# First layer of a retention network with routed experts: the layer-norm rows of four items are written straight into the token rows' place, and GpSimd's two passes over them move four steps later

## The reference

```
xn = layernorm(x)
h = xn
for l in range(4):
    k, q, v = split(h @ Wkqv[l]);  r = tril(q k^T / sqrt(d)) / row_norm;  r = r / clip(|sum r|, 1)
    a, gate = split((r @ v) @ Wm1[l] + bm1[l]);  m = groupnorm(a * silu(gate) @ Wm2[l] + bm2[l])   # per item
    y = m + h
    h = layernorm(gelu(y @ Wf1[l] + bf1[l]) @ Wf2[l] + bf2[l] + y) * ln_g[l] + ln_b[l]
expert = argmax(softmax(xn @ gate_w));  g = weight * (gelu(xn @ w1[e] + b1[e]) @ w2[e] + b2[e])
out = x + h * silu(g)
```

## Time and profile before

| | |
|---|---|
| median of 3 runs | 507.23 us (507.22 to 507.36) |
| the profiled execution | 506.84 us |
| its span | 504.9 us |
| TensorE busy | 469.9 us (93%) |
| VectorE busy | 383.9 us (76%) |
| ScalarE busy | 253.4 us (50%) |
| GpSimd busy | 259.6 us (51%) |
| the multiply L483, 31 times | 42.5 us, 1.37 us each |
| the add L487, 31 times | 41.8 us, 1.35 us each |
| scatters L471, 32 times | 32.5 us, 1.02 us each |

### The profile page before, as it was taken

One profiled execution on the slowest core, in us unless ns is written; L12 is line 12 of the kernel. 1 busy time (PEld: TensorE's weight loads), 2 busy tenths in 40 slices (PEclk: granted clock), 3 DMA queues, 4 the chain that ended last, 5 costly groups with the idle time before them and its releaser, 6 DMA issues.

```text
span 504.9 us, 9876 instructions
## 1 busy us (share of the span) xinstructions
PE 469.9 (93%) x3157; PEld 392.3 (78%) x3157; DVE 383.9 (76%) x1342; ACT 253.4 (50%) x533; POOL 259.6 (51%) x285
## 2 busy tenths in 40 slices
PE   6999889999999999999999999999999999999751
PEld 4887666766889888988888898889888988767431
DVE  4768887788867767777787677777767777889986
ACT  3823334444566554565655446656554565455320
POOL 4520188888454455544545554544455556445542
PEclk9999999999999999999999999999999999999896
DMA  9998411111611111110111111111111000510022
GB/s 264 236 127 204 174 38 39 34 37 58 130 60 43 58 44 59 59 65 31 49 49 51 53 63 59 59 38 38 59 43 59 33 12 6 152 27 1 26 79 62
DMA packets 47345, 35.05 MB, mean 69 GB/s; under 512 B 13320, under 2 KB 38736, under 8 KB 47296
## 3 DMA queue, kind: packets, MB, share of 16 engines
q1 hardware_dynamic: 44496, 28.94, 22.1%
q0 software_dynamic: 2272, 4.71, 2.8%
q10 hardware_dynamic: 528, 0.79, 0.5%
HBM read 14.70 MB, written 9.42 MB: 48 GB/s over the span
## 4 chain that ended last, share of the span: by engine, by line
PE 65%; POOL 12%; DVE 11%; issue 6%; DMA 2%; ACT 1%; POOLq 0%; SPq 0%; DVEq 0%; ACTq 0%
PE bank L1272 8%; PE bank L1199 7%; PE bank L1183 7%; POOL x_slots L471 6%; PE pair L1346 4%; PE pair L1318 4%; PE bank L1210 4%; PE pair L1300 4%; PE bank L1359 4%; PE bank L1211 4%; PE bank L1212 4%; PE pair L1348 3%; PE pair L1298 3%; POOL ln_rs L426 2%; PE bank L1254 2%
## 5 line engine op out<-in xcount | busy, mean ns | idle before, releaser
L483 POOL TENSOR_TENSOR zhat<-zhat,all_lg 128x512 f32<-128x512 f32 x31 | 42.5, 1373 | 88.1 <-PE bank L1244 74.1
L1272 PE MATMUL bank<-all_f,G_sb 128*128 128x128 f32 x512 | 74.2, 278 | 0.0
L656 ACT ACTIVATE y_sb<-bank,gn_bi,gn_sc 128x512 f32<-128x512 f32 x32 | 24.9, 778 | 97.3 <-DVE gn_bi L1050 97.3
L1272 PEld LDWEIGHTS bank<-all_f,G_sb 128*128 128x128 f32 x512 | 68.6, 195 | 1.4 <-issue 1.4
L651 ACT ACTIVATE uT_h<-bank 128x512 fp32r<-128x512 f32 x32 | 19.1, 597 | 97.5 <-PE bank L1254 97.5
L426 POOL TENSOR_TENSOR ln_rs<-ln_ve,half_neg 128x4 f32<-128x4 f32 x32 | 33.4, 1045 | 34.7 <-DVE ln_ve L680 34.4
L1183 PEld LDWEIGHTS bank<-moe_w,h_T 128*128 128x128 f32 x312 | 39.5, 191 | 13.8 <-issue 13.8
L568 ACT ACTIVATE h_T<-bank,w_t 128x128 f32<-128x128 f32 x156 | 44.5, 372 | 5.1 <-PE bank L1199 5.1
L523 POOL DMA_INDIRECT y_rows<-yt,slot_info x39 | 40.9, 1049 | 11.0 <-POOL yt L520 11.0
L636 ACT ACTIVATE G_sb<-bank,all_par 128x512 f32<-128x512 f32 x64 | 43.0, 694 | 7.1 <-PE bank L1235 4.7
L503 POOL TENSOR_TENSOR gn_rs<-gn_ve,half_neg 128x1 f32<-128x1 f32 x32 | 18.5, 578 | 51.4 <-DVE gn_ve L898 51.3
(11 more groups left out here) (178 smaller groups left out, 1241.3 us busy)
## 6 DMA issues: line engine op xcount, KB each, us to landing
w_t<-moe_w SPq DMA_DIRECT2D x39, 258.0 KB, 2.4
x_slots<-moe_w SPq DMA_DIRECT2D x1, 2515.5 KB, 21.6
xt<-x_slots SPq DMA_DIRECT2D x39, 64.0 KB, 1.8
x_sb<-in_L_attn_x SPq DMA_DIRECT2D x8, 256.0 KB, 5.7
moe_w<-in_L_ffn_w SPq DMA_DIRECT2D x1, 2048.0 KB, 19.0
moe_w<-y_rows SPq DMA_DIRECT2D x8, 256.0 KB, 4.6
out<-moe_w SPq DMA_DIRECT2D x7, 256.0 KB, 2.3
all_f<-in_L_attn_Wf SPq DMA_DIRECT2D x2, 512.0 KB, 4.3
```

The source lines that it names most:

```text
L483: pool.tensor_tensor(zhat[:, b % 2, :, :], zhat[:, b % 2, :, :], all_lg[:, li, :].unsqueeze(1).broadcast_to([P, C, D]), ALU.mult)\
L1272: last = mm(bank[7][:, at_c], G_sb[:, k, at_c], all_f2[:, li, k, :], start=False, stop=k == 1)
```

## The change

For items 0 to 3 (`ASIDE`), VectorE and ScalarE write the normalised rows into the item's own place in htok, where TensorE transposes them from (`zhat_rows`). GpSimd's multiply is then in place in htok, and so is the add. These four items' passes leave steps 3 to 6; step 7 has those of items 0 and 4, step 8 of 1 and 5, step 9 of 2 and 6, step 10 of 3 and 7, from step 11 on all is as it was. As htok is made in another order, the waits on its semaphore count by `htok_made`. The three splits of Wf1 leave step 7: each of steps 8, 9 and 10 does one, behind the layer norm's power. Nothing of the computation is altered.

```diff
+        ASIDE = 4
+        HTOK = [k for b in range(ASIDE) for k in (b, ASIDE + b)] + list(range(2 * ASIDE, LB))
+        def htok_made(n):
+            return HTOK.index(n) + 1
+        def zhat_rows(n, b):
+            return htok[:, b * C:(b + 1) * C, 0:D] if n < ASIDE else zhat[:, b % 2, :, :]
...
+            def token_rows(n, b, li):
+                if n < LAST_LAYER:
+                    pool.wait_ge(pe_zT, n + 1)
+                else:
+                    pool.wait_ge(z_done, n + 1)
+                z = zhat_rows(n, b)
+                pool.tensor_tensor(z, z, all_lg[:, li, :].unsqueeze(1).broadcast_to([P, C, D]), ALU.mult)\
+                    .then_inc(hg_done, 1)
+                pool.wait_ge(hg_done, htok_made(n))
+                pool.tensor_tensor(htok[:, b * C:(b + 1) * C, 0:D], z,
+                                   all_lb[:, li, :].unsqueeze(1).broadcast_to([P, C, D]), ALU.add)\
+                    .then_inc(htok_done, 1)
             def step(l, t):
                 first = l == 0
+                s = l * B + t
+                if 0 <= s - (B - 1) < ASIDE:
+                    token_rows(s - (B - 1), s - (B - 1), 0)
                 w = at(l, t, 3, B, LB)
-                if w and w[0] != LB - 1:
...
+                if w and w[0] >= ASIDE and w[0] < LB - 1:
+                    token_rows(*w)
...
-                if first and t == B - 1:
-                    for k in range(1, L - 1):
-                        split_f1(k)
...
-                if first and t == B - 1:
-                    split_f1(L - 1)
+                if l == 1 and t < L - 1:
+                    split_f1(t + 1)
...
-                        last = act.activation(zhat[:, b % 2, c, :], bank[7][:, c * D:(c + 1) * D], ACT.Identity,
+                        last = act.activation(zhat_rows(n, b)[:, c, :], bank[7][:, c * D:(c + 1) * D], ACT.Identity,
...
-                    need(dve, htok_done, n - 1)
+                    if n >= ASIDE + 2:
+                        dve.wait_ge(htok_done, htok_made(n - 2))
...
-                        last = dve.tensor_scalar(zhat[:, b % 2, c, :], bank[7][:, c * D:(c + 1) * D],
+                        last = dve.tensor_scalar(zhat_rows(n, b)[:, c, :], bank[7][:, c * D:(c + 1) * D],
...
-                        last = pe.transpose(bank[7][:, c * P:(c + 1) * P], zhat[:, b % 2, c, :], ident[:, :])
+                        last = pe.transpose(bank[7][:, c * P:(c + 1) * P], zhat_rows(n, b)[:, c, :], ident[:, :])
...
-                        pe.wait_ge(htok_done, n - B + 1)
+                        pe.wait_ge(htok_done, htok_made(n - B))
```

## The result

In the measurement that followed the prediction the changed kernel took **507.91 us** (median of 20 runs, 507.54 to 508.21) beside 507.24 for the kernel before (20 runs): ratio 1.0014, 95% interval 1.0007 to 1.002. That is no change by the bound of 0.2%, 4 us above the predicted 503.9 and outside the range. The same kernel, unaltered, was run three more times while the cause was looked for, each time on another chip, and took **504.69, 504.99 and 504.88 us** (4 runs each) beside 507.21, 507.23 and 507.26 for the kernel before: ratios 0.9947 [0.9931, 0.9964], 0.9955 [0.9938, 0.9971] and 0.9949 [0.9930, 0.9969]. The kernel before takes nearly the same time everywhere (507.0 to 507.3); the changed one does not. So there are two results to explain.

What follows compares the result with a forecast made beforehand. It took GpSimd's queue and the TensorE, VectorE, ScalarE loop as equally long, with passes holding VectorE. 3.64 us gained in steps 3 to 6 less 0.3 in step 8 gave 3.3, so 503.9 us, range 502.2 to 505.8.

Steps and rivals of the forecast that it cites:

- What bounds the kernel: Steps 3 to 6: GpSimd's queue and the TensorE, VectorE, ScalarE loop equally long; passes hold VectorE; step becomes 12.29 us.
- Rival A: Steps 3 to 6: GpSimd's queue is the bound after all, so passes' time comes out until TensorE stops it; 500.3, chance 0.08.
- Steps 3 to 6: Without passes, 0.73 us a step up to u's transpose plus 0.18 at the layer-norm power; 3.64 us over four steps.
- rival D: Steps 3 to 6 keep 13.2 us by a wait replacing L974's, steps 7 to 10 lose nothing; 507.2, chance 0.04.
- Rival B: Steps 3 to 6: scatters take the passes' place and may hold L974; 1.5 us gained, 505.7, chance 0.13.
- Tile 0's first load: Step 7, where L1206 waits 0.48 us for it: nothing gained or lost, could be 0.4 either way.
- Step 7: Item 4's passes end 2.65 us later; L974 may be held but just fits; VectorE's tail up to 0.3 late.
- Step 8: Item 1's multiply makes ln_nb end 0.9 to 1.2 us later, against 0.8 slack; 0.3 lost, bounds 0 and 1.3.
- Steps 9 and 10: Split and two passes fill GpSimd's idle stretch; ln_nb loses 0.17, holds have slack; nothing taken, up to 0.7 a step.
- Rival C: Steps 7 to 10: doubled passes hold VectorE, 5.2 us lost against 3.64 gained; 508.8, decides from 0.91 a step, chance 0.05.
- signs of being wrong: Steps 3 to 6 below 12 us or above 12.6, or steps 8 to 10 growing by more than 0.5 in sum.
- The sum: Whole kernel: 3.64 gained in steps 3 to 6 less 0.3 in step 8, 3.3 us; 503.9 us forecast.

Runs made afterwards that it cites:

- e9: The changed kernel, unaltered, a second time, on another chip than the first result: 504.69 us beside 507.21 for the kernel before.
- e5: The changed kernel with scatters (1, 2, 4) instead of (2, 1, 4), one moved from place 0 to place 1 in steps 3 to 6: 506.30 us.
- e14: The changed kernel without the passes over items 0 to 3 in steps 7 to 10, rerun on another chip: 503.49 us, ratio 0.9928.
- e7: The changed kernel with steps 7 to 11 reordered: item 0's passes behind item 4's, later multiplies and splits mostly behind ln_nb: 503.03 us, ratio 0.9915.
- e1: The changed kernel with the passes over items 0 to 3 left out of steps 7 to 10: 507.34 us beside 507.00.
- e4: The changed kernel with passes of items 0 to 3 behind those of items 4 to 7 and each split behind ln_nb: 509.44 us, ratio 1.0051.
- e6: The kernel before with scatters (1, 2, 4) instead of (2, 1, 4): 507.58 us, ratio 1.0008.
- e8: The changed kernel with steps 7 to 11 reordered as in e7 and scatters (1, 2, 4) besides: 504.48 us, ratio 0.9947.
- e11: The changed kernel with scatters (1, 2, 4), unaltered from e5, a second time on another chip: 506.38 us, ratio 0.9980.
- e3: The kernel before with the place-0 scatters of steps 3 to 6 ahead of GpSimd's two passes: 509.87 us, ratio 1.007.
- e2: The changed kernel with a GpSimd memset of 1280 floats a partition behind the place-0 scatters of steps 3 to 6: 508.57 us, ratio 1.0031.

## Why the prediction was right or wrong

**What bounds the kernel: right.** The two loops are of equal length, and what the passes cost is the hold on VectorE. With the passes gone GpSimd waits, L988 takes 0.22 and the step is 12.2 us in the traces without the delay (L1297 from 84.36 to 96.53 in e9). Rival A, the queue as the bound, would have gone below 12.

**Steps 3 to 6: "From L1254 to the feed-forward product all is VectorE, ScalarE and TensorE in series, and moves along." This is the step that failed in the first result.** It did not move along: gn_m and uT_h started 1.2 and 0.8 us later behind their products than the series allows, 0.8 of the gain of each step went there, and 4.28 - 1.10 = 3.2 us of the 507.91 - 504.69 = 3.2 us between the two medians are this one thing. I had it under rival D as "a wait that takes the place of L974's", with a chance of 0.04, and had named no mechanism for it.

**On the other chips the same step held, and its size was a little low.** From the first statistics instruction to u's transpose 0.73 was forecast, and 0.73 to 0.74 measured in e9. Behind it 0.18 was forecast and 0.30 to 0.38 measured: L694 at 0.17 gives 0.18, and the rest comes from the statistics and ln_nb following a little closer. Together 1.08 a step, 4.3 us, against 3.64.

**Rival B, the scatters take L974's place: no.** L988 took 0.22 in each of steps 3 to 6 in all runs of the changed kernel. e5 shows that the rival was not idle, though, with L694 in its place.

**Tile 0's first load, "nothing gained or lost": half right.** The load's wait went (0.47 gained), but only after 0.98 had been lost ahead of it.

**Step 7: wrong.** I had looked at L974 as what item 0's multiply may hold. It held the gate product before it, 1.93 us long, and TensorE had 0.3 us of slack there. I had put that pass "behind the last scatter" in so many words and had not asked which VectorE instruction runs at the scatter's end: L943 starts 0.17 before it. Net 0.5.

**Step 8: right in mechanism, a little off in size, wrong in price.** ln_nb took 1.15 us instead of 0.33, 0.82 more where "0.9 to 1.2 later" was forecast, about the 0.8 of slack behind it; 0.3 was taken and 0.05 lost, near the lower bound.

**Steps 9 and 10, "Nothing taken; up to 0.7 a step if I misjudge": misjudged.** They lost 0.57 and 0.55. 0.17 of each is ln_nb behind the split, which I had written down and then priced at nothing; by e14 the rest, 0.38, is the passes. It goes over the gate product and the copy L1111 behind it, and this copy is what I had missed: the held instruction had slack, the one queued behind it on VectorE had none. Step 11 loses 0.19 to the third split. Rival C named this mechanism at 1.3 us a step and put the point from which it decides at 0.91; steps 7 to 10 lost 0.51, 0.04, 0.57 and 0.55, so it took 1.7 us of the gain and did not decide. One of the prediction's own signs of being wrong did appear, in all four traces: steps 8 to 10 grew by 1.2 us in sum, against the 0.5 that it allowed.

**The sum.** Forecast 3.64 - 0.3 = 3.3; on the chips without the delay 4.3 - 1.9 = 2.4, by the medians 2.2 to 2.5. The two errors partly cancel: those three results, 504.7 to 505.0, lie within the range, in part by luck, as the loss was 1.9 where 0.3 was taken; the first result does not. The Trainium skill's rule that a VectorE instruction with two SBUF inputs and a GpSimd one on SBUF exclude each other (SBUF — State Buffer, "Who interferes with whom") was borne out in steps 7 to 10 wherever such an instruction met a pass that ran already: L943 1.93 and 1.07, L928 0.80, L700 1.15, L1002 1.22 in e7. What these runs do not bear out is that the later one always waits: L943 was recorded 0.19 us ahead of the multiply that went before it. A_sb, which reads PSUM, took its 0.68 us at 145.64 in the middle of a pass (145.25 to 146.76).

**What stays open.** Why some runs deliver TensorE's signals late. Shown: it comes and goes with the same program. It appeared in the first result and in all four kernels of one chip (e1 to e4), and in none of the thirteen on four other chips, three of the same programs among them. Only nine of these thirteen put it to the test, though. All five kernels that it hit reach the means product without a wait of TensorE and start a scatter 0.54 to 0.56 us ahead of it, and VectorE's reading starts 2.08 to 2.35 us behind the start of that scatter. e6 has the wait, and in e5, e8 and e11 the last scatter starts 1.8 us ahead.

TensorE's signals are not the only ones disturbed. A scatter reports that it is done by 16 updates of a semaphore, its landings. Of the 512 that the 32 scatters make, the five traces with the delay have recorded only 251 to 268, from the first scatter on; each of the other fourteen traces, that of the kernel before among them, has all 512. The view of DMA issues from 60 to 120 us has no time to landing in the first result, and has one in e9:

```profile
x_slots<-xn,pos POOLq DMA_INDIRECT x32
```

```profile
x_slots<-xn,pos POOLq DMA_INDIRECT x32, 2.3
```

In step 4 of the first result no update of any semaphore is recorded from 85.47 to 86.65; that of L1297 follows at 86.69 and that of L1269 at 86.75. In this stretch from 60 to 120 us the longest such silence is 1.18 to 1.26 us in the five traces and 0.75 in each of the other fourteen. Part of a silence may be updates that are only missing from the record: L988's is missing too, and TensorE took its result in time at 85.16. And not every scatter delays a reader: in the same step 4 L968 reads the product L1363 at 95.23, 0.03 us behind its end and 1.5 behind the start of a scatter. So a rival is left: that on such a chip it takes a scatter close ahead of the product. (1, 2, 4) moves that scatter, and it was not run there.

In those stretches the granted clock was 1.00 in both cases, and the scatters' starts, durations and packets stood at the same distances from L1297. That it is the chip itself and not its condition at the time was not shown, since no chip came up twice. On the chip that delayed e1 to e4 the program counts too: the kernel before took 507.0 us there (no trace of it is kept from there), and e3, which differs from it in the place of the scatters alone, has the delay. That edit does two things at once: it frees L974, so that TensorE comes to L1282 without a wait, and it puts a scatter 0.54 us ahead of L1282, where the kernel before has its last one 3.7 us ahead. Which of the two counts was not separated. e2's and e4's edits did not cure the delay there, and no other was tried on that chip as a cure.

## What to carry to other kernels

A moved GpSimd pass has two prices: the VectorE instruction with two SBUF inputs that it holds, and whatever is queued behind that one. Look up, for the exact microsecond where the pass will start, what VectorE does there and who is next. Put such a pass behind an instruction that is known to be past (a wait on ln_nb, as in e7) and not behind the power that feeds it: the same eight passes and three splits then cost nothing by step 11 (4.19 us early against 4.24 in step 7) instead of 1.9 us.

When a difference of half a per cent is traced through experiments, repeat the kernel in question on every chip, and not only the kernel before. The kernel before took 507.0 to 507.3 us on every chip and so said that the groups could be compared; three theories on scatters and idle engines were built on a difference that lay between two chips.

## What the runs showed of the hardware

- A TensorE result can reach its readers 0.8 to 1.4 us late while TensorE's own rows stay the same. In steps 3 to 6 of five traces VectorE started 1.53 to 1.81 us behind the start of a 0.28 us product instead of 0.32 (0.72 in step 3), and ScalarE 1.45 to 1.71 behind the u transposes instead of 0.67, the two 0.06 us apart. No trace of the same kernels on other chips has it. The same five traces lack about half of the scatters' landings; none of the others lacks any.
- GpSimd can win the handoff at the end of its own instruction. L943, recorded from 119.15, 0.17 before a scatter's end, was overtaken by the multiply behind the scatter (119.34 to 120.53) and ended at 121.08; L700, 0.03 behind the power, ended at 130.72, a pass later. Between a multiply and its own add it did not: L943 ended 0.55 behind the multiply, and the add took 1.51 us, against 1.18 where it met nothing (at 130.77).
- A scatter holds even a VectorE instruction with one SBUF input and 4 elements a partition: L694 0.40 us in e5, L680 0.35 before, 0.17 free.
